# Spills of converted weight blocks: from GpSimd's software queue to SyncE's hardware queue, one slot later

## What is computed

```
x = x + xattn(ctx, layernorm(x), ...)   # queries from 64 latents, keys and values from 512 context rows + latents, 8 heads
x = x + attn(layernorm(x), ...)         # differential attention among the 64 latents
x = x + ffn(layernorm(x), ...)          # gate, up, down; activations and weights quantised to 4 bits in blocks of 16

def fp4_quant_dequant(x):               # for the activations and for w_gate, w_up (1408x512), w_down (512x1408)
    scale = max(max(|x_block|) / 6, 1e-12)
    return GRID[searchsorted(MID, |x / scale|)] * sign(x) * scale
```

## Time and profile before

| | us |
|---|---|
| median of 3 runs (lowest, highest) | 995.66 (992.62, 996.56) |
| the profiled execution's own time | 999.49 |
| its span, first to last instruction | 997.7 |
| PE busy | 954.4 (96%) |
| DVE busy | 772.9 (77%) |
| ACT busy | 440.2 (44%) |
| POOL busy | 144.9 (15%) |
| mean granted TensorE clock | 0.995 of 2.4 GHz |

### The profile page before, as it was taken

One profiled execution on the slowest core, in us unless ns is written; L12 is line 12 of the kernel. 1 busy time (PEld: TensorE's weight loads), 2 busy tenths in 40 slices (PEclk: granted clock), 3 DMA queues, 4 the chain that ended last, 5 costly groups with the idle time before them and its releaser, 6 DMA issues.

```text
span 997.7 us, 16573 instructions
## 1 busy us (share of the span) xinstructions
PE 954.4 (96%) x6364; PEld 776.7 (78%) x6364; DVE 772.9 (77%) x1653; ACT 440.2 (44%) x848; POOL 144.9 (15%) x166
## 2 busy tenths in 40 slices
PE   5999899999999979999999999999999999999997
PEld 4778788787888868787888887777777678888885
DVE  6555677798788858887887884578888588999984
ACT  4533654664465445466446644633324322222221
POOL 1220011211111111111211211022322000000000
PEclk9999999999999999999999999999999999999999
DMA  5788576756667563685676557160001730000000
GB/s 213 197 251 186 160 143 151 164 111 181 162 111 183 136 164 99 155 169 118 169 155 148 120 141 184 39 222 23 1 1 59 289 118 11 11 11 11 11 11 21
DMA packets 91994, 120.04 MB, mean 120 GB/s; under 512 B 47366, under 2 KB 56198, under 8 KB 89612
## 3 DMA queue, kind: packets, MB, share of 16 engines
q1 hardware_dynamic: 83980, 93.30, 32.7%
q0 software_dynamic: 7360, 24.65, 13.2%
q10 hardware_dynamic: 576, 1.05, 0.3%
HBM read 89.04 MB, written 29.93 MB: 119 GB/s over the span
## 4 chain that ended last, share of the span: by engine, by line
PE 65%; DVE 15%; DMA 7%; issue 6%; ACT 5%; POOL 1%; SPq 0%; DVEq 0%; ACTq 0%
PE ps_banks L146 16%; PE ps_banks L148 15%; PE ps_banks L147 15%; PE ps_banks L462 5%; DMA scratch_rstd<-sb_rstd_b 4%; PE ps_banks L580 3%; PE ps_banks L661 3%; PE ps_banks L728 2%; PE ps_banks L729 2%; PE ps_banks L730 2%; DVE sb_kfull L894 1%; DVE sb_kT_lo L865 1%; DMA scratch_wdn<-sb_w_lo 1%; DVE sb_b_stats L826 1%; PE ps_banks L495 1%
## 5 line engine op out<-in xcount | busy, mean ns | idle before, releaser
L1430 ACT ACTIVATE sb_kT_hi<-sb_kfull 128x512 fp32r<-128x512 f32 x64 | 40.5, 632 | 164.5 <-DVE sb_kfull L894 164.5
L146 PE MATMUL ps_banks<-sb_zT_hi,sb_wkv_hi 128*128 128x512 f32 x256 | 106.9, 418 | 0.3 <-DVE sb_kfull L894 0.3
L148 PE MATMUL ps_banks<-sb_zT_hi,sb_wkv_lo 128*128 128x512 f32 x256 | 100.9, 394 | 0.0
L147 PE MATMUL ps_banks<-sb_zT_lo,sb_wkv_hi 128*128 128x512 f32 x256 | 100.4, 392 | 0.0
L147 PE MATMUL ps_banks<-sb_wkv_lo,sb_zT_hi 128*128 128x512 f32 x256 | 100.3, 392 | 0.0
L146 PE MATMUL ps_banks<-sb_wkv_hi,sb_zT_hi 128*128 128x512 f32 x256 | 100.1, 391 | 0.0
L148 PE MATMUL ps_banks<-sb_wkv_hi,sb_zT_lo 128*128 128x512 f32 x256 | 100.0, 390 | 0.0
L945 DVE CUSTOM_DVE_ANT_0 sb_probs<-ps_banks,sb_maskbias 128x576 f32<-128x576 f32 x64 | 48.1, 751 | 34.1 <-PE ps_banks L148 33.7
L146 PE MATMUL ps_banks<-sb_wgu,sb_z_hi 128*128 128x512 f32 (+1 forms) x192 | 73.7, 384 | 0.0
L147 PE MATMUL ps_banks<-sb_wgu,sb_z_hi 128*128 128x512 f32 (+1 forms) x192 | 72.1, 375 | 0.0
L148 PE MATMUL ps_banks<-sb_wgu,sb_z_lo 128*128 128x512 f32 (+1 forms) x192 | 72.0, 375 | 0.0
(11 more groups left out here) (263 smaller groups left out, 2435.3 us busy)
## 6 DMA issues: line engine op xcount, KB each, us to landing
sb_ctx<-in_ctx SPq DMA_DIRECT2D x16, 1024.0 KB
sb_ctxT<-in_ctx_t SPq DMA_DIRECT2D x16, 1024.0 KB, 8.4
sb_wgu<-scratch_wgu SPq DMA_DIRECT2D x8, 1024.0 KB, 9.7
scratch_wgu<-sb_w_hi POOLq DMA_DIRECT2D x22, 256.0 KB
scratch_wgu<-sb_w_lo POOLq DMA_DIRECT2D x22, 256.0 KB
sb_wdn<-scratch_wdn SPq DMA_DIRECT2D x2, 2816.0 KB, 9.7
scratch_q<-sb_a_qk POOLq DMA_DIRECT2D x8, 512.0 KB, 7.2
sb_rstd_row<-scratch_rstd SPq DMA_DIRECT2D x16, 256.0 KB, 4.8
```

What stands on the lines that cost most here:

```text
L146: e.matmul(o, wh, xh, start=i == 0, stop=False)
L147: e.matmul(o, wh, xl, start=False, stop=False)
L148: m = e.matmul(o, wl, xh, start=False, stop=i == n - 1)
L1430: e.activation(dst, src, ACT.Identity).then_inc(done)
```

## The change

`spill_weight` moves, unchanged, from POOL's program to SP's. POOL called it in the slot of the job's split. SP calls it in the slot after that (the variable `turned` carries the job over), behind everything else that SP's list has up to that slot, and ahead of a weight load of the same slot. PE's, ACT's and DVE's programs are as they were, and so are the bytes moved and the semaphores.

```diff
@@ POOL: pool_program
-            def spill_weight(job):
-                kind, g, r, c0, width = JOBS[job]
-                k = width // P
-                bank, nth = took["w", job]
-                on.wait_ge(drained[bank], nth)
-                for part, src in enumerate((w_hi, w_lo)):
-                    dst = wgu_spill[g, part, :, :, r * P:(r + 1) * P] if kind == "gu" else \
-                        wdn_spill[part, :, c0 // P:c0 // P + k, r * P:(r + 1) * P]
-                    copy_bits(e, dst, src[:, 0:k, :]).then_inc(w_spilled, 16)
...
-                    for job, step in WEIGHTS.get((b, slot), ()):
-                        if step == SPLIT_STEP:
-                            spill_weight(job)
@@ SP: sync_program
+            def spill_weight(job):
...
+            turned = None
             for b in range(NB + 1):
...
+                    if turned is not None:
+                        spill_weight(turned)
+                    turned = None
                     for job, step in WEIGHTS.get((b, slot), ()):
+                        if step == SPLIT_STEP:
+                            turned = job
                         if step == TURN_STEP and job + 2 < NJ:
                             load_weight(job + 2)
```

More of the change, by code:

```diff
@@ L2038, in load_weight @@
                 copy_bits(e, w_in[job % 2][:, 0:width], src).then_inc(w_in_landed[job % 2], 16)
+            def spill_weight(job):
+                kind, g, r, c0, width = JOBS[job]
+                k = width // P
+                bank, nth = took["w", job]
+                on.wait_ge(drained[bank], nth)
+                for part, src in enumerate((w_hi, w_lo)):
+                    dst = wgu_spill[g, part, :, :, r * P:(r + 1) * P] if kind == "gu" else \
+                        wdn_spill[part, :, c0 // P:c0 // P + k, r * P:(r + 1) * P]
+                    copy_bits(e, dst, src[:, 0:k, :]).then_inc(w_spilled, 16)
             def load_d_weight(n):
```

## The result

| | before | after |
|---|---|---|
| median of 4 runs each on one chip, us (lowest, highest) | 995.6 (992.62, 996.56) | 1009.36 (1006.81, 1014.76) |
| the profiled execution's own time, us | 999.49 | 1011.28 |
| its span, us | 997.7 | 1009.5 |

The ratio after to before is 1.015, with a 95% interval from 1.01 to 1.0201. (It compares the means of the runs; the medians alone are 1.4% apart.) The change makes the kernel slower by 1.5%. The forecast was 1005 us, 0.9% slower.

A forecast was written before the change was run, and what follows sets the result against it. PE, busy 96% of the span, bounds the kernel; 15.0 us of new PE waits minus 6.9 gained is 8.1 slower. 999.49 + 8.1 = 1007.6, less 2.6 gives 1005 us; range 1001 to 1012, 8-in-10 range 992 to 1017.

The forecast's parts named there:

- The sign, the place and the number of places: PE waits before its transposes of the probabilities (L462) in seven places; the kernel gets 8.1 us slower net.
- The wait for the small numbers: On SP, `sb_rstd_row` starts 9.9 us after the small spill, bounds 9.4 and 13.1, holding up the spill behind it.
- The landing: The spill pair lands 6.4 us after the start of `sb_rstd_row`, bounds 3.8 and 11.0.
- Rival B: It balances: landing 1.2 us sooner, 7.8 us lost against 8.1 gained, about 999 on the profile's scale; chance 0.22.
- PE's waits: PE idles 2.5 us in each of six batches, 15.0 us; in the seventh, 23.8 us becomes 18.9, gaining 4.9.
- The clock: The half clock behind PE's old 7.1 us wait goes, 2.0 us gained.
- rival C: More places give way: late spills or packs, 14 us more, or half clock after each wait, 12 more; chance 0.16, shared.
- Packs, context and weight blocks: Loads queued behind the spills on SP: a spill pair costs them 1.8 us, but PE loses 0.
- POOL's 11 us: POOL's 11.0 us wait before the second spill DMA of job 15 is removed if it belongs to POOL's way of starting DMAs.
- rival D: The 11 us wait is the memory's and SP gets it too: nothing gained, 1014.5 us; chance within a shared 0.16.
- Rival A: Spill and `sb_rstd_row` overlap, landing in 3.8 us, so PE is on time: 9.1 us gained, 990.4 us; chance 0.15.
- The step from profile to median: The profiled execution lay 3.8 us above the median; 2.6 of it is taken off, turning 1007.6 into 1005 us.

The follow-up runs named there:

- Experiments 1: The changed kernel with `sb_rstd_row` put behind the spill in SP's list: 992.18 us against 993.41 for the kernel before, ratio 0.9992.
- 5: The changed kernel with `sb_rstd_row` put behind the spill in odd batches alone: 1000.06 us against 1004.05 for the kernel before, ratio 0.9947.
- experiment 2: The kernel before, spills on POOL, which in slots 4 and 5 first waits for the small numbers to be written: 1038.23 us against 993.41, ratio 1.0445.
- 3: The changed kernel with a second pair of buffers for odd jobs below 28: 987.19 us against 993.41 for the kernel before, ratio 0.993.
- experiment 9: The changed kernel with two buffer pairs, late start on SP: 985.48 us against 1000.3 for the kernel before, ratio 0.9858.
- experiments 6: The kernel before, spills on POOL, with a second pair of buffers for odd jobs up to 27: 996.77 us against 1004.05, ratio 0.993.
- 7: The changed kernel with two buffer pairs and the spill ahead of `sb_rstd_row` on SP: 998.64 us, ratio 0.9937 to the kernel before.

## Why the prediction was right, and where it was off

- **The sign, the place and the number of places** were right. PE waits seven times, in front of L462, for `sb_w_lo`. Experiments 1 and 5 (start early: the loss goes), 2 (start late on the other queue: a loss comes) and 3 (nobody waits: the loss goes) show each link of the chain. One reading of the start was short: ACT also waited three times, 6.0 us, for the spills of w_down (`scratch_wdn`), beside the five waits of 21.1 us that the prediction names. Nothing in the sum used it.
- **The wait for the small numbers** was put at 9.9 us, and it is 11.1 in batch 1 and 9.0 to 11.1 in the seven odd batches.
- **The landing** was put at 6.4 us from the start of `sb_rstd_row`; ACT went on 161.28 - 156.18 = 5.1 us after it. The two errors cancel in batch 1, which is luck: the forecast had the spill down 1.1 + 9.9 + 6.4 = 17.4 us after the load of `sb_ctx`, and ACT goes on after 17.3. **Rival B** had the landing right (1.2 us sooner, that is 5.2) but it kept the 9.9, and so had PE 1.2 us too early, and it left the half clock out.
- **PE's waits** were put at 2.5 us in each of six places, and at 7.1 - 4.9 = 2.2 in the seventh; the mean of all is 15.2 / 7 = 2.2. Against it the 7.1 us of the long wait are gone. Two traces of each kernel show how wide this is: 15.2 and 20.7 us after, 7.1 and 5.4 before.
- **The clock** is the term that was wrong, in sign and in size. I took 2.0 us as gained, since the half clock had stood only behind the longest wait, and put the loss behind the new waits into rival C, at 12 us. The 2.0 us for the old stretch were right (4.2 / 2 = 2.1). But in the first trace of after PE's work at half speed costs 15.8 / 2 = 7.9, so there is a loss of 4.4 (from the busy time) to 5.8 us in place of the gain. In the second trace PE is busy in 25.0 of the 27.3 us, which is 12.5. The one row that I had gave no ground to assume that shorter waits go without it. This part of rival C was true: it named 12 us, and the two traces show 7.9 and 12.5.
- **Packs, context and weight blocks** were counted as 0. PE's lists of waits in both traces of after name no DMA, so none of them reached it. In batch 3 the last pack starts at 201.60 and lands 5.3 us later, at 206.9, and the first scores that want it come at 209.82:

```profile
201.60 2.68 SPq L131 DMA_DIRECT2D sb_vlpack<-scratch_vlat  x1
...
209.82 0.29 PE L146 MATMUL ps_banks<-sb_kT_hi,sb_qpack 128*128 128x288 f32 x1
```

- **POOL's 11 us** went, and they were POOL's: rival D is refuted, since no such stand came on SP. The rule of the Trainium skill that I weighed (page SBUF — State Buffer, section SBUF: two separate sides), by which such a wait disappears with SyncE as the starter, held for the wait. As a forecast of the time it failed, because the wait was worth less than the new place in SP's list costs. Whether VectorE's lock is its cause is not shown: in the three traces with one pair of buffers it stood at the same two DMAs, and the rule names nothing that would single these two out.
- **Rival A** wanted the spill down 3.8 us after the start of `sb_rstd_row`. It took 5.1, and the small numbers took 1.2 us more than the 9.9, so PE came 2.5 us later than A has it (18.8 against 16.3).
- **The small waits for `sb_tile_lo`**, 4.6 us before, were not in the sum at all. They fell by 3.6 us, which is what kept the total near the forecast.
- **The step from profile to median**, -2.6 us, had no ground. The executions of one kernel differ by 3.9 us in the first stage alone. Without it the forecast is 1007.6, against 1011.28 in the profiled execution and 1009.36 in the median.

In one sum for the profile: forecast +8.1, made of +10.1 of waits (15.0 - 4.9) and -2.0 of clock. Found in the stage, for the same matmuls, +8.5, made of +4.1 of idle time (+8.1, -3.6 and -0.4) and +4.4 of slower work. The mechanism of the waits was right. That the totals agree within 0.4 us is luck, since the idle time came out 6.0 us lower than forecast and the clock term 6.4 us higher. The 3.7 us by which the profile lies above 1007.6 are the 3.0 of the first stage, the 0.3 of the rest, and these 0.4.

## What to carry to other kernels

An engine that only starts transfers is still an in-order list: before a DMA is moved to it, look for the longest wait that it would stand behind (here a round trip of 512 small numbers through memory, 9 to 11 us), and for who waits for its landing. A late start cost nothing here once a second buffer stood between the landing and the next writer, and that buffer (0.7 to 1.4% gained) was worth more than the choice of queue. And where PE is the bound, price new idle stretches of 2 us with a half clock at some of them (here at 11 of 14, 3.4 or 6.8 us long), not with their own length alone.

## What the runs showed that I had not expected

- **The clock at short waits.** With PE waits of 1.5 to 3.3 us, a stretch of 3.4 or 6.8 us at half clock stood at four of seven in one execution, and with waits of 2.1 to 3.9 us at seven of seven in another. It begins inside the wait or up to 1.1 us behind it. A wait of 1.96 us had none and one of 1.92 had. In experiment 9 one of 2.3 us had none.
- **POOL's queue stands at fixed places.** The waits without a visible reason come at the second DMA of jobs 15 and 31, 32 DMAs of POOL apart: 11.0 and 7.3 us, and again 9.7 and 6.8. In experiment 2, where these DMAs come later, they were 5.9 and 3.3. With two buffer pairs it was 0.5 at the first place, and the second wait, of 11.8 to 13.0, came near 575 us, at the first DMA of job 31 and not at its second. The cause stays open.
- **Small writes are slow, and a large one beside them is too.** In the odd batches of after, the spill of 512 numbers of 4 bytes took 9.0 to 11.1 us until it was reported. The 512 KB of a weight job's spill, started 2 us behind it, took 156.44 - 144.28 = 12.2 us in before, and 4.7 us in after, where it started behind their end. That the small writes cause this, and not the 1 MB load of `sb_ctx` that runs at the same time, was not tested.
- **The slower queue from a late start.** From the same late start the pair takes 8.2 us on POOL's queue and 4.7 on SP's, though with an early start and two pairs the two queues give equal times (experiments 6 and 7). The one pair of landings was not isolated from what else ran.
